# Pair grams in fp32, one sample in a quarter of the array, in place of split fp32r grams of four samples

## The chip, the cores and the metric
The kernel runs on one core of one Trainium2 chip. The metric is the device time of one execution in microseconds. The times shown are medians of a few executions, and the profile is of one more execution, whose own time is given beside its span.

## The reference
The program is a recommendation model: dot products between all pairs of 27 feature vectors of a sample, followed by a small multilayer perceptron. Biases are not zero.

```python
# bottom_output (2048, 27, 128), bottom_mlp_output (2048, 128), all float32
dots  = jnp.einsum('bfd,bgd->bfg', bottom_output, bottom_output)
pairs = dots[:, tril_i, tril_j]                    # 351 pairs below the diagonal
x = jnp.concatenate([bottom_mlp_output, pairs, zeros(B, 1)], axis=1)   # 480 columns
for w, b in ((w0, b0), (w1, b1), (w2, b2), (w3, b3)):   # 480 -> 1024 -> 1024 -> 512 -> 256
    x = jax.nn.relu(x @ w.T + b)
return x @ w_out.T + b_out                          # (2048, 1)
```

## The kernel before
The batch is cut into 8 chunks of 256 samples. A chunk passes through the four layers with its samples as the 256 moving columns of each product (`products`, L776). Each layer product is made of three fp32r products: high weights by high activations, low weights by high activations, high weights by low activations (`ALL`; `HIGH` is the first two). A chunk has 136 tile products of each kind, 408 matmuls. ScalarE drains an accumulator with bias and relu (`drain`, L891), VectorE rounds the result to fp32r (`split_high`, L1022), and GpSimd subtracts to get the low part (`split_low`, L626).

While a chunk goes through the layers, the pair products ("grams") of the next chunk are made beside it. A gram is the 27 x 27 matrix of dot products of one sample. Four samples are a group, four groups a unit, 16 units a chunk. A unit goes through this chain:

- SP loads its rows (`load_rows`, L500), in four DMAs of 32-row blocks, arranged so that VectorE's transposes of 32 x 32 blocks turn them whole.
- VectorE transposes (`turn_raw`, L977) into `raw`, with features in the columns: 128 partitions (the 128 dimensions) x 512.
- ScalarE rounds to fp32r (`turned_hi`, L863); VectorE subtracts for the low part (`turned_lo`, L982; in chunk 0 every second unit's is on GpSimd, L619).
- TensorE makes four products, one a group (`gram`, L735): the weights are the high parts of 4 samples in 128 columns, the moving columns are 4 x 28 of the high parts and as many of the low parts. That computes all cross products of four samples, of which only the four diagonal 27 x 27 blocks are wanted. Each unit takes two banks of PSUM, and there are two such pairs (`GRAM_RING`, `GRAM_BANKS`).
- ScalarE copies three of the four samples' blocks, high by high and high by low, out of PSUM into `parts` (`gram_parts`, L875), VectorE the fourth (`gram_parts_rest`, L1004).
- VectorE transposes the high-by-low parts (`turn_low`, L1015), GpSimd adds them twice, once as they are and once transposed (`add_parts`, L605 and L612), into `grams`.

When the 16 units of a chunk are there, SP spills `grams` to memory (`spill`, L447) and gathers the wanted pairs back as 351 rows of 256 samples (`gather`, L452). They are split into high and low parts at the end of the chunk (`pairs_hi`, L901, `pairs_lo`, L1050).

The first chunk's grams come ahead of everything (`first_steps`). There the rows are turned by TensorE (`turn_early`, L691), copied by ScalarE (L848), and each group's gram is one plain fp32 product of 108 columns by 128 weight columns (`gram_early`, L715). ScalarE and VectorE share the copies out of PSUM (`early_move`, L856, `early_rest`, L991). Then the weights are transposed by TensorE (`turn_weights`, L686) through the same PSUM banks and split by ScalarE (L840) and VectorE (L968). Some of that stands in the middle of chunk 0.

The order of the work is written out once for all engines. `chunk_steps` makes a list of steps, and each engine runs through the same list and does its own part. `hooks_of` gives small lists of steps ("hooks") that are put in after every 18 matmuls of the layers (`HOOK`; in chunk 0 after every 6, a unit every second hook). What a hook holds is made by `unit_steps(n, ahead)`: the transpose of unit n, the split of unit n - 1, the gram of unit n - 3 and the sum of unit n - 4. The first five hooks' worth of a chunk stand at the end of the chunk before it (`AHEAD`), so a chunk c does most units of chunk c + 1 and begins those of c + 2. Each engine executes its instructions in order, with semaphore waits between them. Chunk 7 has no grams beside it.

Of the kernel before, what the change touches and what calls it, by code (L numbers as in the profile page):

```python
# [14 lines left out]
P = 128  # L15
# [39 lines left out]
ACC_RING, GRAM_RING, TURN_RING = 3, 2, 2  # L55
GRAM_BANKS = 2

XT_RING, XT_LAG = 4, 2
assert ACC_RING + 1 + GRAM_RING * GRAM_BANKS == 8

# [9 lines left out]
EVEN = FEATS + 1  # L70
EARLY_SLOTS, SHORT_LAG = 8, 2
RAW_RING = 2
EARLY_XT = 2 * XT_RING
EARLY_BY_ACT = [1] * (UNITS - 4) + [2] * 4
QUADS_BY_ACT = 3
# [59 lines left out]
def unit_steps(n, ahead):  # L135


    steps, g = [], n - 1 - XT_LAG
    if n < UNITS:
        steps.append(("raw", ahead, n))  # L140
    if 1 <= n <= UNITS:
        steps.append(("turn", ahead, n - 1))
    if g >= 1:
        steps.append(("sum", ahead, g - 1))
    if g >= 0:
        steps.append(("gram", ahead, g))
    if g == UNITS - 1:
        steps.append(("sum", ahead, g))
    return steps


UNIT_HOOKS = UNITS + XT_LAG + 1
# [92 lines left out]
def dlrm_program(nc, x, x_mlp, w0, b0, w1, b1, w2, b2, w3, b3, w_out, b_out, y):  # L245
    weights = [w0, w1, w2, w3]
    biases = [b0, b1, b2, b3]
    with ExitStack() as ctx:
# [28 lines left out]
        raw = sb("raw", [P, RAW_RING, UNIT_GROUPS, GROUP * QUAD])  # L277
        mlp_rows = sb("mlp_rows", [P, 2, P])
        xt_full, = shared(("xt_full", [P, EARLY_XT, UNIT_GROUPS, GROUP * QUAD]))
        xt = sb("xt", [P, XT_RING, UNIT_GROUPS, 2, GROUP * QUAD], F32R)  # L280
        parts = sb("parts", [P, 2, 2, UNIT_GROUPS, QUAD])
        low_t = sb("low_t", [P, 2, UNIT_GROUPS, QUAD])
# [11 lines left out]
        gram_ps = ctx.enter_context(nc.psum_tensor("gram_ps", [P, GRAM_RING * GRAM_BANKS, 512], F32))  # L294
# [13 lines left out]
        grams_zeroed = sem("grams_zeroed")  # L308
        xt_zeroed = sem("xt_zeroed")
        parts_zeroed = sem("parts_zeroed")  # L310
# [4 lines left out]
        raw_turned = sem("raw_turned")  # L315
        xt_hi_done = sem("xt_hi_done")
        xt_done = sem("xt_done")
        xt_odd_done = sem("xt_odd_done")
        gram_done = sem("gram_done")
        early_moved = sem("early_moved")  # L320
        parts_done = sem("parts_done")
        parts_rest_done = sem("parts_rest_done")
        low_turned = sem("low_turned")
        sum_done = sem("sum_done")
# [60 lines left out]
        def weight_bank(n):  # L385

            return gram_ps[:, n % (GRAM_RING * GRAM_BANKS), :] if n < LATE_WEIGHTS else side_ps[:, :]

# [5 lines left out]
        def by_pool(d, u):  # L394

            return isinstance(d, int) and d == 1 and u % 2 == 1

        def wait_xt(engine, d, u):

            if isinstance(d, int) and u < 0:  # L400
                d, u = d - 1, u + UNITS
            if by_pool(d, u):
                engine.wait_ge(xt_odd_done, u // 2 + 1)
            elif isinstance(d, int) and d <= 1:
                engine.wait_ge(xt_done, d * UNITS + (u // 2 if d else u) + 1)
            else:
                engine.wait_ge(xt_done, d * UNITS - UNITS // 2 + u + 1)

        def xt_part(u, h):

            return xt[:, u % XT_RING, :, h, :].rearrange("p j (s f) -> p j s f", s=GROUP)[:, :, :, 0:FEATS]

        def early_xt(u):

            return xt_full[:, u % EARLY_XT].rearrange("p j (s f) -> p j s f", s=GROUP)[:, :, :, 0:FEATS]

        def early_gram(u, s):

            found = gram_ps[quad_of(s), u % (GRAM_RING * GRAM_BANKS), 0:UNIT_COLS].rearrange("p (j n) -> p j n", j=UNIT_GROUPS)
            return found[:, :, FEATS * s:FEATS * (s + 1)]  # L420

        def gram_place(u, s):

            return grams[quad_of(s), :, u * UNIT_GROUPS:(u + 1) * UNIT_GROUPS].rearrange("p g j -> p j g")

        def raw_cols(u):

            return raw[:, u % RAW_RING].rearrange("p j (s f) -> p j s f", s=GROUP)[:, :, :, 0:FEATS]

# [3 lines left out]

        def quad_of(s):

            return slice(QUAD * s, QUAD * s + FEATS)

        def gram_found(u, s):

            b = u % GRAM_RING * GRAM_BANKS  # L440
            found = gram_ps[quad_of(s), b:b + GRAM_BANKS, :].rearrange("p a (b n) -> p (a b) n", n=2 * P)
            return found[:, :, 0:2 * GROUP * EVEN].rearrange("p j (h n) -> p h j n", h=2)[
                :, :, :, EVEN * s:EVEN * s + FEATS]

# [32 lines left out]
        def _(sp):  # L477
# [28 lines left out]
            def spill(d, quads=range(GROUP)):  # L506


                sp.wait_ge(grams_done, d * UNITS + UNITS)
                if isinstance(d, int) and d == 0:  # L510
                    sp.wait_ge(early_moved, UNITS)
                for s in quads:
                    spill_quad(sp, s)
# [68 lines left out]
        def _(pool):  # L582
# [6 lines left out]
            nc.gpsimd.memset(grams[:], 0.0).then_inc(grams_zeroed, 1)  # L589
# [8 lines left out]

            def add_parts(d, u):

                n = (d - 1) * UNITS + u + 1
                hh, hl = parts[:, u % 2, 0], parts[:, u % 2, 1]
                pool.wait_ge(parts_done, n)
                pool.wait_ge(parts_rest_done, n)
                nc.gpsimd.tensor_tensor(hh, hh, hl, ALU.add).then_inc(sum_done, 1)  # L605

                pool.wait_ge(sum_done, n)
                pool.wait_ge(low_turned, n)
                if u == 0:

                    pool.wait_ge(spilled, d * GROUP * 16)
                nc.gpsimd.tensor_tensor(  # L612
                    grams[:, :, u * UNIT_GROUPS:(u + 1) * UNIT_GROUPS].rearrange("p g j -> p j g"),
                    parts[:, u % 2, 0, :, 0:FEATS], low_t[:, u % 2, :, 0:FEATS], ALU.add).then_inc(grams_done, 1)

            def turned_lo(d, u):

                pool.wait_ge(xt_hi_done, (d - 1) * UNITS + u + 1)
                nc.gpsimd.tensor_tensor(xt_part(u, 1), raw_cols(u), xt_part(u, 0).bitcast(F32),  # L619
                                        ALU.subtract).then_inc(xt_odd_done, 1)  # L620
# [8 lines left out]
            def chunk(c):  # L629
                for step in steps_of(c):  # L630
                    if step[0] == "mm":
                        _, layer, m, _, k1, parts = step
                        if k1 == K_TILES[layer] and 2 in parts and layer < 3:
                            split_low(c, layer, m)
                    elif step[0] == "turn" and by_pool(c + step[1], step[2]):
                        turned_lo(c + step[1], step[2])
                    elif step[0] == "sum":
                        add_parts(c + step[1], step[2])
# [9 lines left out]
        def _(pe):  # L648
            def turn_weights(n):

                g, bank, ring = ORDER[n], weight_bank(n), GRAM_RING * GRAM_BANKS
                if n < ring:

                    pe.wait_ge(early_moved, UNITS + 1 - ring + n)
# [48 lines left out]
            def gram_early(u):  # L703


                pe.wait_ge(xt_done, u + 1)
                if u == 0:
                    pe.wait_ge(xt_zeroed, 1)
                ring = GRAM_RING * GRAM_BANKS
                if u >= ring:  # L710

                    pe.wait_ge(early_moved, u + 1 - ring)
                    pe.wait_ge(grams_done, u + 1 - ring)
                for j in range(UNIT_GROUPS):
                    last = nc.tensor.matmul(gram_ps[:, u % ring, j * GROUP_ROWS:(j + 1) * GROUP_ROWS],  # L715
                                            xt_full[:, u % EARLY_XT, j, :], early_xt(u)[:, j], start=True, stop=True)
                last.then_inc(gram_done, 1)

            def gram(d, u):

                wait_xt(pe, d, u)
                if isinstance(d, int) and d == 1 and u < GRAM_RING:
                    if u == 0:

                        pe.wait_ge(w_done, LATE_WEIGHTS)
                        pe.wait_ge(xt_zeroed, 2)
                else:

                    pe.wait_ge(parts_done, (d - 1) * UNITS + u + 1 - GRAM_RING)
                    pe.wait_ge(parts_rest_done, (d - 1) * UNITS + u + 1 - GRAM_RING)  # L730
# [83 lines left out]
            for step in first_steps():  # L814
                if step[0] == "turn":
                    turn_early(step[1])
                elif step[0] == "early":
                    gram_early(step[1])
# [13 lines left out]
        def _(act):  # L832
# [10 lines left out]
            def early_copy(u):  # L843
                act.wait_ge(turned, u + 1)
                if u >= EARLY_XT:

                    act.wait_ge(gram_done, u + 1 - EARLY_XT)
# [273 lines left out]
```

## Time and profile before

| | us |
|---|---|
| median of 3 runs | 517.59 (516.37 to 517.98) |
| the profiled execution | 519.78 |
| its span, first to last instruction | 518.0 |
| first and last instruction of the early grams' matmuls on TensorE | 5.6 to 28.2 |
| one steady chunk | 57 |
| mean granted TensorE clock, share of full | 0.984 |
| DMA traffic | 53.24 MB |

The kernel before is also measured beside every later run. A row of a group has the line of the kernel, the engine (PE is TensorE's matmul, PEld its weight load, DVE is VectorE, ACT ScalarE, POOL GpSimd, SP SyncE, with a q for the sequencer that issues DMAs), the operation, what it writes and reads, the shapes and the count. Behind the first bar stand the busy time in us and the mean ns of one; behind the second the time for which the engine was idle just before them, and what ended it. Matmuls overlap in the pipeline, so that their busy time is less than count times mean, and the distance from one start to the next is the cost of one. Weight loads overlap with matmuls.

### The profile page before, as it was taken

What the parts mean: (1) busy time and instruction counts of PE and PEld (TensorE: products, weight loads), DVE (VectorE), ACT (ScalarE), POOL (GpSimd) and SP (SyncE); (2) the same over time, 40 slices, a digit from 0 to 9 for tenths busy, and PEclk for the clock granted to TensorE, in tenths of its full rate; (3) what the DMA queues carried; (4) which work ended last, traced back from release to release, by engine and by line L of the source; (5) the groups of instructions that cost most, each with busy time, mean ns of one, the idle gap of its engine ahead of it and who ended that gap; (6) DMA issues with size and microseconds to landing.
All of it is one profiled execution on the core that took longest, in us unless ns stands there. A gap on an engine that the chain in (4) does not pass through costs nothing.

```text
span 518.0 us, 13822 instructions
## 1 busy us (share of the span) xinstructions
PE 495.9 (96%) x4075; PEld 488.7 (94%) x4075; DVE 322.2 (62%) x742; ACT 295.9 (57%) x736; POOL 263.9 (51%) x475
## 2 busy tenths in 40 slices
PE   6986998898999999999999999999999999999998
PEld 6975997898999999999999999999999999999997
DVE  3764778665884788648974788458874788332110
ACT  4654677853864577637773586547763686433112
POOL 2710377632865367624864287626764386524221
PEclk9986999998999999999999999999999999999999
DMA  8997877447673566347663666266653762210000
GB/s 220 235 307 163 261 120 120 69 93 119 98 110 72 106 113 100 62 107 120 102 101 68 113 106 106 50 124 113 101 81 83 129 96 41 57 41 2 1 1 0
DMA packets 281055, 53.24 MB, mean 103 GB/s; under 512 B 265126, under 2 KB 279230, under 8 KB 281022
## 3 DMA queue, kind: packets, MB, share of 16 engines
q1 hardware_dynamic: 279090, 52.22, 53.2%
q10 hardware_dynamic: 1932, 0.61, 0.5%
q8 instruction: 17, 0.28, 0.2%
q14 instruction: 16, 0.13, 0.1%
HBM read 45.71 MB, written 7.09 MB: 102 GB/s over the span
## 4 chain that ended last, share of the span: by engine, by line
PE 79%; DMA 6%; issue 4%; POOL 3%; SPq 3%; ACT 3%; DVE 1%; ACTq 0%; POOLq 0%; DVEq 0%
PE acc L776 67%; PE gram_ps L735 8%; DMA blocks<-grams 2%; DMA rows<-in_r_bottom_output_dram 2%; PE gram_ps L715 2%; DMA pairs<-blocks 1%; ACT parts L875 1%; POOL parts L605 1%; SPq L482 1%; ACT h_full L891 1%; PE gram_ps L686 1%; POOL grams L612 1%; POOL xt L619 1%; SPq L447 1%; SPq L452 1%
## 5 line engine op out<-in xcount | busy, mean ns | idle before, releaser
L776 PE MATMUL acc<-h_a,w_hi 128*128 128x256 f32 x1152 | 223.7, 285 | 3.4 <-DVE h_a L1022 2.4
L776 PEld LDWEIGHTS acc<-h_a,w_hi 128*128 128x128 f32 x1152 | 185.2, 191 | 5.2 <-DVE h_a L1022 3.0
L891 ACT ACTIVATE h_full<-acc,small_t 128x256 f32<-128x256 f32 x175 | 82.9, 473 | 148.0 <-PE acc L776 146.6
L776 PE MATMUL acc<-h_a,w_lo 128*128 128x256 f32 x576 | 158.7, 282 | 0.0
L626 POOL TENSOR_TENSOR h_a<-h_full,h_a 128x256 fp32r<-128x256 f32 x96 | 72.2, 752 | 135.0 <-DVE h_a L1022 135.0
L875 ACT ACTIVATE parts<-gram_ps 27x216 f32<-27x216 f32 x336 | 114.4, 340 | 41.3 <-PE gram_ps L735 27.6
L776 PEld LDWEIGHTS acc<-h_a,w_lo 128*128 128x128 f32 x576 | 110.2, 191 | 0.0
L776 PE MATMUL acc<-x,w_hi 128*128 128x256 f32 x504 | 102.8, 291 | 2.4 <-ACT x L901 2.4
L776 PE MATMUL acc<-h_b,w_hi 128*128 128x256 f32 x512 | 97.2, 284 | 0.0
L776 PEld LDWEIGHTS acc<-x,w_hi 128*128 128x128 f32 x504 | 84.4, 197 | 3.4 <-ACT x L901 3.1
L977 DVE STREAM_TRANSPOSE raw<-rows 128x512 f32<-128x512 f32 x112 | 78.9, 704 | 7.4 <-DMA rows<-in_r_bottom_output_dram 4.2
L626 POOL TENSOR_TENSOR h_b<-h_full,h_b 128x256 fp32r<-128x256 f32 x64 | 47.4, 740 | 69.9 <-DVE h_b L1022 69.9
L776 PEld LDWEIGHTS acc<-h_b,w_hi 128*128 128x128 f32 x512 | 81.6, 191 | 0.0
L605 POOL TENSOR_TENSOR parts<-parts 128x128 f32<-128x128 f32 x112 | 77.5, 692 | 5.6 <-DVE parts L1004 5.1
L982 DVE TENSOR_TENSOR xt<-raw,xt 128x432 fp32r<-128x432 f32 x104 | 74.6, 717 | 1.0 <-ACT xt L863 1.0
L776 PE MATMUL acc<-x,w_lo 128*128 128x256 f32 x252 | 72.0, 289 | 0.0
L1022 DVE CAST h_a<-h_full 128x256 fp32r<-128x256 f32 x96 | 30.2, 314 | 64.1 <-ACT h_full L891 62.4
L776 PE MATMUL acc<-h_b,w_lo 128*128 128x256 f32 x256 | 70.0, 283 | 0.0
L735 PE MATMUL gram_ps<-xt 128*128 128x224 f32 x448 | 67.9, 274 | 0.3 <-POOL xt L619 0.3
L863 ACT ACTIVATE xt<-raw 128x432 fp32r<-128x432 f32 x112 | 62.6, 559 | 2.7 <-DVE raw L977 2.2
L1022 DVE CAST h_b<-h_full 128x256 fp32r<-128x256 f32 x64 | 18.8, 294 | 67.9 <-ACT h_full L891 67.7
L612 POOL TENSOR_TENSOR grams<-parts,low_t 128x108 f32<-128x108 f32 x112 | 47.9, 427 | 25.3 <-DVE low_t L1015 13.4
(67 smaller groups left out, 488.7 us busy)
## 6 DMA issues: line engine op xcount, KB each, us to landing
rows<-in_r_bottom_output_dram SPq DMA_DIRECT2D x444, 64.0 KB, 2.1
blocks<-grams SPq DMA_DIRECT2D x30, 216.0 KB, 4.0
w_raw<-in_L_rec_w_dram SPq DMA_DIRECT2D x6, 1024.0 KB, 7.3
early_rows<-in_r_bottom_output_dram SPq DMA_DIRECT2D x12, 224.0 KB, 6.1
stage_pairs<-in_L_rec_w_dram SPq DMA_DIRECT2D x1, 1408.0 KB, 10.2
w_raw<-in_L_rec_w_dram SPq DMA_DIRECT2D x2, 512.0 KB, 8.9
mlp_rows<-r_bottom_mlp_output_dram SPq DMA_DIRECT2D x8, 128.0 KB, 2.2
pairs<-blocks SPq DMA_DIRECT2D x8, 126.0 KB
```

Source lines behind the costliest of these rows:

```text
L605: nc.gpsimd.tensor_tensor(hh, hh, hl, ALU.add).then_inc(sum_done, 1)
L612: nc.gpsimd.tensor_tensor(grams[:, :, u * UNIT_GROUPS:(u + 1) * UNIT_GROUPS].rearrange("p g j -> p j g"), parts[:, u % 2, 0, :, 0:FEATS], ...
L626: nc.gpsimd.tensor_tensor(h[:, m, 1, :], h_full[:, slot % 2, :], h[:, m, 0, :].bitcast(F32), ALU.subtract).then_inc(split_done, 1)
L715: last = nc.tensor.matmul(gram_ps[:, u % ring, j * GROUP_ROWS:(j + 1) * GROUP_ROWS], xt_full[:, u % EARLY_XT, j, :], early_xt(u)[:, j], st ...
L735: last = nc.tensor.matmul(found, xt[:, u % XT_RING, j, 0], both, start=True, stop=True)
L776: last = nc.tensor.matmul(acc_slot(c, slot), weight(wp, layer, m, k), in_tile(layer, k, xp), start=(k == 0 and n == 0), stop=(k == K_TILES ...
L863: nc.scalar.activation(xt_part(u, 0), raw_cols(u), ACT.Copy).then_inc(xt_hi_done, 1)
L875: last = nc.scalar.activation(parts[quad_of(s), u % 2, :, :, 0:FEATS], gram_found(u, s), ACT.Copy)
L891: nc.scalar.activation(h_full[:, slot % 2, :], acc_slot(c, slot), ACT.Relu, bias=small_t[:, slot:slot + 1]).then_inc(drained, 1)
L977: nc.vector.transpose(raw[:, u % RAW_RING].rearrange("p j n -> p (j n)"), rows[:, r].rearrange("p j n -> p (j n)")).then_inc(raw_turned, 1)
L982: nc.vector.tensor_tensor(xt_part(u, 1), raw_cols(u), xt_part(u, 0).bitcast(F32), ALU.subtract).then_inc(xt_done, 1)
L1022: nc.vector.tensor_copy(h[:, m, 0, :], h_full[:, slot % 2, :]).then_inc(high_done, 1)
```

## The change
All grams, the early ones too, become plain fp32 products of one sample: the weights are that sample's 32 columns (27 features and 5 zeros), the moving columns its 27 features, and the product is placed in the 32-column quarter of the array that ends in the sample's 32 partitions of PSUM. A unit becomes 16 products in one bank (`GRAM_RING` is 4 banks now), and its gram leaves the bank in one copy of 128 x 108 elements, by ScalarE in the steady chunks and by VectorE in the early ones. VectorE's transpose writes straight into `xt`, a ring of 8. `raw`, `parts`, `low_t`, `xt_full`, the split of x, the sum on GpSimd, the memset of `grams` and their semaphores are gone. A hook holds the transpose of unit n and the gram of unit n - 1, so a chunk needs 17 hooks in place of 19. In a chunk's first unit ScalarE waits for the spill of the chunk before it, as GpSimd did.

```diff
-ACC_RING, GRAM_RING, TURN_RING = 3, 2, 2
-GRAM_BANKS = 2
-
-XT_RING, XT_LAG = 4, 2
+ACC_RING, GRAM_RING, TURN_RING = 3, 4, 2
+
+XT_RING, XT_LAG, UNIT_LAG = 8, 2, 1
...
-    steps, g = [], n - 1 - XT_LAG
+    steps = []
     if n < UNITS:
         steps.append(("raw", ahead, n))
-    if 1 <= n <= UNITS:
-        steps.append(("turn", ahead, n - 1))
-    if g >= 1:
-        steps.append(("sum", ahead, g - 1))
-    if g >= 0:
-        steps.append(("gram", ahead, g))
-    if g == UNITS - 1:
-        steps.append(("sum", ahead, g))
+    if n >= UNIT_LAG:
+        steps.append(("gram", ahead, n - UNIT_LAG))
     return steps
...
+        def samples(u):
+            return xt[:, u % XT_RING].rearrange("p j (s f) -> p j s f", s=GROUP)[:, :, :, 0:FEATS]
+        def gram_found(u):
+            return gram_ps[:, u % GRAM_RING, 0:P].rearrange("p (j f) -> p j f", f=QUAD)[:, :, 0:FEATS]
+        def gram_place(u):
+            return grams[:, :, u * UNIT_GROUPS:(u + 1) * UNIT_GROUPS].rearrange("p g j -> p j g")
...
-                    sp.wait_ge(raw_turned, (d - 1) * UNITS + u + 1 - ROWS_RING)
+                    sp.wait_ge(xt_done, d * UNITS + u + 1 - ROWS_RING)
...
+            def gram(d, u):
+                pe.wait_ge(xt_done, d * UNITS + u + 1)
+                if isinstance(d, int) and d == 0 and u == 0:
                     pe.wait_ge(xt_zeroed, 1)
...
+                elif not (isinstance(d, int) and d == 0 and u < GRAM_RING):
+                    pe.wait_ge(grams_done, d * UNITS + u + 1 - GRAM_RING)
                 for j in range(UNIT_GROUPS):
-                    at = j % 2 * 2 * P
-                    found = gram_ps[:, u % GRAM_RING * GRAM_BANKS + j // 2, at:at + 2 * GROUP * EVEN]
-                    both = xt[:, u % XT_RING, j].rearrange("p h (s f) -> p (h s) f", f=QUAD)[:, :, 0:EVEN]
-                    last = nc.tensor.matmul(found, xt[:, u % XT_RING, j, 0], both, start=True, stop=True)
+                    for s in range(GROUP):
+                        at = slice(QUAD * s, QUAD * (s + 1))
+                        last = nc.tensor.matmul(gram_found(u)[at, j], xt[:, u % XT_RING, j, at], samples(u)[:, j, s],
+                                                start=True, stop=True, tile_position=(0, QUAD * s))
                 last.then_inc(gram_done, 1)
...
+            def move_gram(d, u):
+                act.wait_ge(gram_done, d * UNITS + u + 1)
                 if u == 0:
+                    act.wait_ge(spilled, d * GROUP * 16)
+                nc.scalar.activation(gram_place(u), gram_found(u), ACT.Copy).then_inc(grams_done, 1)
...
+                dve.wait_ge(gram_done, d * UNITS + u + 1 - XT_RING)
+                nc.vector.transpose(xt[:, u % XT_RING].rearrange("p j n -> p (j n)"),
+                                    rows[:, r].rearrange("p j n -> p (j n)")).then_inc(xt_done, 1)
+            def early_move(u):
                 dve.wait_ge(gram_done, u + 1)
+                nc.vector.tensor_copy(gram_place(u), gram_found(u)).then_inc(grams_done, 1)
```

## Rows read from the trace of the kernel before

**Rows 1.** The page's head: busy time of each engine over the whole span.
```profile
PE 495.9 (96%) x4075; PEld 488.7 (94%) x4075; DVE 322.2 (62%) x742; ACT 295.9 (57%) x736; POOL 263.9 (51%) x475
```

**Rows 2.** By stretch: length, busy PE, PEld, DVE, ACT, POOL; clock, DMA share, GB/s.
```profile
62.00:121.00 59.00, 52.71 (x436) 51.03 (x434) 41.25 (x93) 40.43 (x103) 34.45 (x56) 1.00 0.62 105
121.00:178.00 57.00, 56.41 (x463) 56.35 (x464) 39.24 (x90) 33.27 (x85) 32.52 (x52) 0.97 0.56 97
...
406.00:463.00 57.00, 56.80 (x478) 56.49 (x477) 35.01 (x84) 32.88 (x86) 32.21 (x51) 1.00 0.41 73
```

**Rows 3.** The chain of waits: start us, us, what; early units, first spill, steady chunk.
```profile
18.06 0.89 PE gram_ps L715 x8
...
25.81 2.69 PE gram_ps L715 x24
...
30.09 8.53 DMA blocks<-grams
...
171.72 2.87 PE acc L776 x24
```

**Rows 4.** Timeline of TensorE's matmuls: start us, us from first start to last end.
```profile
199.77 0.60 PE L735 MATMUL gram_ps<-xt 128*128 128x224 f32 x4
200.21 0.29 PE L776 MATMUL acc<-h_a,w_hi 128*128 128x256 f32 x1
...
202.37 0.60 PE L735 MATMUL gram_ps<-xt 128*128 128x224 f32 x4
```

**Rows 5.** Groups of instructions by line, costliest first: busy us, mean ns, idle before.
```profile
L776 PE MATMUL acc<-h_a,w_hi 128*128 128x256 f32 x1152 | 223.7, 285 | 3.4 <-DVE h_a L1022 2.4 <-ACT h_full L891 1.0
...
L875 ACT ACTIVATE parts<-gram_ps 27x216 f32<-27x216 f32 x336 | 114.4, 340 | 41.3 <-PE gram_ps L735 27.6 <-POOL grams L612 10.3
...
L891 ACT ACTIVATE h_full<-acc,small_t 128x256 f32<-128x256 f32 x175 | 82.9, 473 | 148.0 <-PE acc L776 146.6
...
L977 DVE STREAM_TRANSPOSE raw<-rows 128x512 f32<-128x512 f32 x112 | 78.9, 704 | 7.4 <-DMA rows<-in_r_bottom_output_dram 4.2 <-POOL xt L619 2.6
...
L863 ACT ACTIVATE xt<-raw 128x432 fp32r<-128x432 f32 x112 | 62.6, 559 | 2.7 <-DVE raw L977 2.2
...
L715 PE MATMUL gram_ps<-xt_full 128*128 128x108 f32 x128 | 18.3, 293 | 0.0
...
L856 ACT ACTIVATE grams<-gram_ps 27x108 f32<-27x108 f32 x20 | 7.0, 350 | 6.8 <-PE gram_ps L715 6.7
...
L750 PE MATMUL side_ps<-ident,mlp_rows 128*128 128x128 f32 x16 | 3.0, 272 | 0.0
...
L791 PE MATMUL side_ps<-h_full,small_t 128*1 128x256 f32 x4 | 1.0, 377 | 0.2 <-ACT h_full L891 0.2
...
L791 PEld LDWEIGHTS side_ps<-h_full,small_t 128*1 128x1 f32 x4 | 0.2, 80 | 0.7 <-issue 0.4 <-ACT h_full L891 0.3
```

**Rows 6.** The chain of waits in chunk 0: start us, us, what.
```profile
82.76 0.96 POOL xt L619
...
108.06 4.03 DMA blocks<-grams
```

**Rows 7.** Timeline of the weight loads at the end of the kernel.
```profile
514.67 0.11 PEld L791 LDWEIGHTS side_ps<-h_full,small_t 128*1 128x1 f32 x2 [0.35 <-issue]
515.09 0.13 PEld L791 LDWEIGHTS side_ps<-h_full,small_t 128*1 128x1 f32 x2 [0.30 <-ACT h_full L891]
```

**Rows 8.** Timeline of all engines at the start of one steady unit.
```profile
199.65 0.28 PE L776 MATMUL acc<-h_a,w_hi 128*128 128x256 f32 x1
199.65 0.19 PEld L735 LDWEIGHTS gram_ps<-xt 128*128 128x128 f32 x1
```

**Rows 9.** Timeline of matmuls where transposes stand between products.
```profile
171.34 0.38 PE L750 MATMUL side_ps<-ident,mlp_rows 128*128 128x128 f32 x2
171.47 0.36 PE L776 MATMUL acc<-h_b,w_hi 128*128 128x256 f32 x1
171.67 0.28 PE L776 MATMUL acc<-h_b,w_lo 128*128 128x256 f32 x1
```

More of the change, by code:

```diff
@@ L385, in weight_bank @@
         def weight_bank(n):
[L387 removed]
+            return gram_ps[:, n % GRAM_RING, :] if n < LATE_WEIGHTS else side_ps[:, :]
         def raw_rows(n):
@@ L634, in chunk @@
                             split_low(c, layer, m)
[L635 to L638, printed above, removed]
             chunk(0)
@@ L701, in turn_early @@
                 turn_rows(u, early_rows_of(u))
-            def gram_early(u):
-                pe.wait_ge(xt_done, u + 1)
-                if u == 0:
+            def gram(d, u):
+                pe.wait_ge(xt_done, d * UNITS + u + 1)
+                if isinstance(d, int) and d == 0 and u == 0:
                     pe.wait_ge(xt_zeroed, 1)
[L709 to L721, printed above, removed]
                 if isinstance(d, int) and d == 1 and u < GRAM_RING:
@@ L817, in _ @@
                 elif step[0] == "early":
-                    gram_early(step[1])
+                    gram(0, step[1])
                 elif step[0] == "weights":
@@ L916, in chunk @@
                             drain(c, layer, m)
-                    elif step[0] == "turn":
-                        turned_hi(c + step[1], step[2])
                     elif step[0] == "gram":
-                        gram_parts(c + step[1], step[2])
+                        move_gram(c + step[1], step[2])
                     elif step[0] == "weights":
@@ L932, in _ @@
                     early_copy(step[1])
-                elif step[0] == "early":
-                    early_move(step[1])
                 elif step[0] == "spill":
                     act.wait_ge(grams_done, UNITS)
-                    act.wait_ge(early_moved, UNITS)
                     for s in (2, 3):
@@ L985, in early_rest @@
-            def early_rest(u):
-                dve.wait_ge(gram_done, u + 1)
-                if u == 0:
-                    dve.wait_ge(grams_zeroed, 1)
-                for s in range(EARLY_BY_ACT[u], GROUP):
-                    last = nc.vector.tensor_copy(gram_place(u, s), early_gram(u, s))
-                last.then_inc(grams_done, 1)
-            def gram_parts_rest(d, u):
-                dve.wait_ge(gram_done, d * UNITS + u + 1)
-                if isinstance(d, int) and d == 1 and u < 2:
-                    dve.wait_ge(parts_zeroed, 1)
-                else:
-                    dve.wait_ge(grams_done, d * UNITS + u - 1)
-                for s in range(QUADS_BY_ACT, GROUP):
-                    last = nc.vector.tensor_copy(parts[quad_of(s), u % 2, :, :, 0:FEATS], gram_found(u, s))
-                last.then_inc(parts_rest_done, 1)
@@ L1007, in turn_low @@
-            def turn_low(d, u):
-                n = (d - 1) * UNITS + u + 1
-                dve.wait_ge(parts_done, n)
-                dve.wait_ge(parts_rest_done, n)
-                if not (isinstance(d, int) and d == 1 and u < 2):
-                    dve.wait_ge(grams_done, d * UNITS + u - 1)
-                nc.vector.transpose(low_t[:, u % 2].rearrange("p j g -> p (j g)"),
-                                    parts[:, u % 2, 1].rearrange("p j g -> p (j g)")).then_inc(low_turned, 1)
+                dve.wait_ge(gram_done, d * UNITS + u + 1 - XT_RING)
@@ L1063, in chunk @@
                         turn_raw(c + step[1], step[2])
-                    elif step[0] == "turn" and not by_pool(c + step[1], step[2]):
-                        turned_lo(c + step[1], step[2])
-                    elif step[0] == "gram":
-                        gram_parts_rest(c + step[1], step[2])
-                    elif step[0] == "sum":
-                        turn_low(c + step[1], step[2])
                     elif step[0] == "weights":
@@ L1075, in chunk @@
                         pairs_lo(c + step[1])
-            nc.vector.memset(xt_full.rearrange("p r j (s f) -> p (r j s) f", f=QUAD)[:, :, FEATS:], 0.0).then_inc(xt_zeroed, 1)
-            nc.vector.memset(parts[:], 0.0).then_inc(parts_zeroed, 1)
+            nc.vector.memset(xt.rearrange("p r j (s f) -> p (r j s) f", f=QUAD)[:, :, FEATS:], 0.0).then_inc(xt_zeroed, 1)
             for step in first_steps():
                 if step[0] == "early":
-                    early_rest(step[1])
+                    early_move(step[1])
                 elif step[0] == "weights":
```

117 lines of the change are left out of this document (8 added, 109 removed).

## Prediction
> **What bounds the kernel now.** I read the page's head first: TensorE is busy 96% of the span, the other engines 51 to 62% [rows 1]. A busy share alone does not say that TensorE sets the time, so I took the busy time by stage next [rows 2]. In a steady chunk of 57 us (there are six, from 121 to 463 us) TensorE is busy 56.4 to 56.8; from 62 to 121 it idles 6.3 us (59.0 less 52.7); before that it waits for the first transfers. From 463 us on there are no grams, and nothing there changes. The granted clock is 0.97 to 1.00 in these rows.
>
> The chain of waits [rows 3] confirms it: in a steady chunk it runs through L776 and L735 on TensorE, a product of 256 columns taking 0.120 us (24 in 2.87). The timeline shows the grams of one unit from 199.77 to 200.21, then 18 products to 202.37, then the next unit [rows 4]. **A unit costs 0.44 us of TensorE; with 18 products of 0.12 it makes the period of 2.60 us.** All that the other engines do per unit lies beside it. So the question is whether 16 small fp32 products fit into 0.44 us.
>
> **The change, part by part.** From the other engines it takes much. Per unit ScalarE loses 0.56 + 3 x 0.34 us [rows 5], VectorE three of its four instructions, GpSimd both. ScalarE gains one copy out of a bank, 128 x 108 elements; the nearest row is L856, the same layout on 27 partitions, 0.35 us. All of it lies under a period of 2.6 us and is worth only the stalls that those engines cause: the 6.3 us of idle TensorE in chunk 0, where the chain passes GpSimd's L619 [rows 6], and some 0.2 us per steady chunk. Part of chunk 0's idle time belongs to weight turning, which stays. I take 6 us, bounds 0 and 8. The dropped memset of grams lies ahead of a wait for weights, and is worth nothing; so is the shorter evacuation after the last early gram, under the rounding.
>
> On TensorE the trace has one thing to go by: an fp32 product is issued as two loads and two matmuls (128 records at L715 for the 64 products of 16 units [rows 5]). So a unit becomes 32 load/matmul pairs in place of 4. **What does a pair cost?** Three limits follow from rows.
>
> (a) Streaming. L791 (256 columns, fp32) takes 0.377 us a record where L776 (256 columns, fp32r) takes 0.285 [rows 5]. The 0.092 more is near the 0.107 of another 256 columns at 2.4 GHz, so an fp32 pass streams at about two cycles a column, and 27 columns take 54 / 2.4 = 22.5 ns.
>
> (b) Loading. At L715 eight pairs take 0.89 us, 0.111 each [rows 3], although by (a) their 108 columns stream in 0.090. So the load of 128 columns bounds there. Two cycles a column are 0.107, so 0.004 is fixed, and 32 columns need 64 / 2.4 + 4 = 31 ns.
>
> (c) The turn from one set of weights to the next. With one weight column, at L791, the second load starts 0.03 us after the first in one pair and 0.05 in the other: 0.11 and 0.13 less a record of 0.08 [rows 5, 7]. The matmul starts between them.
>
> (b) and (c) say 31 to 33 ns; a straight line from (c)'s first pair to (b)'s 128 columns says 33 + 31 x 0.61 = 52. I take 33, since a fixed 33 ns added to a rate of 0.83 ns a column would overshoot the measured 0.111. The last gram is followed by a load of 128 columns that a matmul of 22 ns can't cover: 0.11 once. **Unit: 31 x 0.033 + 0.111 = 1.13 us, against 0.44: +0.69.**
>
> That happens 7 x 16 = 112 times: +77 us. The 16 early units take 0.89 us each (8 records' steps) [rows 3]: +0.24 each, exposed for the nine from 18 us on, where TensorE carries the chain: +2.2. The seven before lie beside the arriving rows.
>
> Moved waits. The gram now waits for a transpose of one hook earlier (0.70 us, L977), before for a split of two hooks earlier. TensorE queues everything behind that wait, and reaches the next hook after 2.16 + 1.13 = 3.3 us; in that time VectorE must see a drain (0.47), cast it and transpose, under 2 us together: hidden. In chunk 0 a unit comes every 12 products, 2.6 us, beside the weight copies; at worst the saving there is lost, which is the bound of 0. Before a chunk's first gram is copied, ScalarE instead of GpSimd now waits for the spill, and its drains queue behind. That spill starts after unit 15, six hooks earlier, and lands in 4 to 8.5 us [rows 3, 6]: hidden. SP's row loads wait for the same transposes as before, and neither SP nor GpSimd issues another DMA.
>
> The sum: 519.8 (profiled; span 518.0) + 77 + 2.2 - 6 = 593. The median of 517.6 is 2.2 lower, so 590.8, **590 us**.
>
> **Two rules beside the rows.** Between a transpose by the array (L750) and a 256-column product the timeline shows no stop: the second L750 starts at 171.44 (0.38 less 0.27 [rows 5] after 171.34), the second product at 171.67, and 0.23 is just their two steps, 0.11 and 0.12 [rows 9]. The sum therefore charges nothing for a change of shape. The Trainium skill, "TensorEngine Tiling (Array Packing)", section Tiling Modes, says that changing the tiling mode drains TensorE; no row of before enters a tiling mode, so the trace can't confirm it. Two such changes a unit are rival 3.
>
> The closest matmul starts of these rows are 171.44 and 171.47. The Trainium skill, "TensorE: Matmul & The Clock Gate", section Back-to-back issue gap, puts the least start-to-start at about 25 ns, which agrees; by it even perfectly overlapped quarters would need 31 x 0.025 + 0.11 = 0.89 us a unit, an estimate of 562 in all. With matmuls decoded in software it gives 62 ns each, an estimate of 2.03 us a unit and some 700 in all.
>
> **The rivals.**
> 1. *Quarters overlap.* Another quarter loads and streams while one works; only the turn from first to second pass within a product stays serial. 16 x 0.033 + 0.08 = 0.61 us a unit: +0.17 x 112 = 19, early -2.5, stalls -6: 528. Half way to the serial case, at 0.87 us: 560. For it: the four products of a group share nothing but x. Against: a load starts only when the matmul before it does, both at 199.65 [rows 8]. Chance 0.22. The same page on the clock gate, Part 3, says that tiles run concurrently.
> 2. *Serial*, as summed: 0.36.
> 3. *Each change of array shape drains.* A record at L776 lasts 0.285, of which 0.107 is streaming, so 0.18 is the way through the array. Twice a unit 0.36; for 121 units +44: 634. Chance 0.17.
> 4. *The turn grows with the columns*, 52 ns a pair: 1.72 us a unit, +143, early +7.5, -6: 662. A lower granted clock in stretches of narrow products would land here too. Chance 0.12.
> 5. *A 32-column load takes as long as 128 columns*, the quarter buying nothing: 32 x 0.111 = 3.55 a unit, +348, +24, -6: 884. Chance 0.04.
> 6. *Faster.* All quarters run at once through both passes: 32 x 0.033 / 4 + 0.08 = 0.34 us. TensorE saves 0.10 x 112 + 0.55 x 9, and 6 of stalls: 495. It decides once a unit takes less than about 0.52 us (112 x 0.08 = 6 + 9 x 0.37), near 13 ns a pair, less than half of any step between starts shown above. Chance 0.06; between this and rival 1 lies no change, 0.03.
>
> **The numbers.** Within 0.3%, 1.6 us, a measurement here can't tell a change from none. Slower 0.36 + 0.22 + 0.17 + 0.12 + 0.04 = 0.91, same 0.03, faster 0.06. The range takes in rivals 1 and 3 and the lower part of 4: 530 to 655 us. Below it lie rival 6, no change and the very end of rival 1 (0.10), above it rival 5 and half of rival 4 (0.10).
>
> **What would show it.** In the changed profile: a steady chunk of some 68 us (57 + 16 x 0.69) in place of 57; 3584 + 512 matmul records for grams; in the timeline 1.1 us from a unit's first gram to the next product, matmul starts 0.033 apart, and a first product that comes a full load late. Rival 1 would show starts 33 and then a few ns apart in turn; rival 3 a hole of 0.18 us before and after the grams; rival 4 even steps of 50 ns. TensorE stays busy in over 97% of a steady chunk, ScalarE falls to a third or less. The idle time of chunk 0 should be nearly gone. I am wrong if a steady chunk takes under 60 us, or if TensorE waits for VectorE's transposes.

## The result and the profile after

The changed kernel takes 541.2 us (539.35 to 542.35), the kernel before 516.98 beside it: a ratio of 1.045, 95% interval 1.041 to 1.049. The direction was forecast; the size was not: +24 us in place of +73, and made of other parts.

The page's head of the kernel after, to set against [rows 1]: TensorE has nearly twice the matmul records (7595 against 4075) and only 13 us more busy time, while the other three engines have lost about half of theirs, as expected.

```profile
PE 508.7 (94%) x7595; PEld 479.5 (89%) x7595; DVE 171.5 (32%) x384; ACT 166.6 (31%) x380; POOL 132.8 (25%) x242
```

Busy time by stage, the same view as [rows 2] (length, then busy PE, PEld, DVE, ACT, POOL, the granted clock, DMA):

```profile
62.00:121.00 59.00, 58.08 (x1033) 54.54 (x1034) 26.96 (x52) 22.35 (x51) 11.26 (x15) 1.00 0.68 118
...
182.00:243.00 61.00, 58.63 (x924) 55.54 (x923) 19.43 (x44) 17.77 (x43) 15.00 (x20) 1.00 0.55 94
243.00:304.00 61.00, 60.22 (x924) 57.10 (x924) 17.87 (x40) 17.08 (x42) 14.97 (x20) 0.97 0.54 91
```

Chunk 0 is nearly full now: 0.9 us idle in that window where it was 6.3. But a steady window, which was full before, has a hole of 2.4 us. The chain of waits gives the length of a chunk from the one pair of transposes in each (start us, us, what):

```profile
168.09 0.22 PE side_ps L642 x2
...
229.90 0.22 PE side_ps L642 x2
...
293.35 0.22 PE side_ps L642 x2
...
356.31 0.22 PE side_ps L642 x2
```

That is 61.8, 63.5 and 63.0 us, against 56.9 to 57.2 before; I had forecast 68. The waits of TensorE and the timeline at the start of a chunk name the hole:

```profile
PE acc L668 <- issue: 11.6, 4, 3.1
```
```profile
178.18 0.64 PE L668 MATMUL acc<-h_a,w_hi 128*128 128x256 f32 x4
181.74 0.38 PE L668 MATMUL acc<-x,w_hi 128*128 128x256 f32 x1 [2.92 <-issue]
```

The last product of chunk 1 and the first of chunk 2 are 3 us apart, and "issue" says that nothing which the profile shows was waited for. There are four such holes, and a loop of five iterations turns four times. A unit of grams, in the timeline of the matmuls, against [rows 4]:

```profile
200.40 0.28 PE L668 MATMUL acc<-h_a,w_hi 128*128 128x256 f32 x1
200.61 0.45 PE L626 MATMUL gram_ps<-xt 128*32 128x27 f32 x32
200.99 0.39 PE L668 MATMUL acc<-h_a,w_hi 128*128 128x256 f32 x1
201.22 0.28 PE L668 MATMUL acc<-h_a,w_lo 128*128 128x256 f32 x1
```

From the last product before the grams to the second one after them are 0.82 us; less two steps of 0.12, **the unit costs 0.58 us**. The same reading of before (199.65 to 200.34) gives 0.45. And inside the 0.58 the 32 matmuls are all started within 0.45 - 0.19 = 0.26 us (the record of one is 192 ns here), 8.4 ns from start to start. The rest is at the edges: 0.09 us between the end of the product's step (200.52) and the first gram, and 0.12 from the last gram's start (200.87) to 200.99, where the full-width product's load begins; that load then takes its 0.11 uncovered.

So two things were to be explained: 8.4 ns where I had 33, and holes that I hadn't foreseen.

### The profile page after: what moved, and what is told of

Read it like the earlier page. It is cut to its first block, busy times and chain, and to the rows that moved or that the text cites. A ratio compares the mean times of both kernels' runs of the same rounds, so it can differ in the third digit from the quotient of the medians.

```text
span 539.3 us, 18870 instructions
## 1 busy us (share of the span) xinstructions
PE 508.7 (94%) x7595; PEld 479.5 (89%) x7595; DVE 171.5 (32%) x384; ACT 166.6 (31%) x380; POOL 132.8 (25%) x242
## 4 chain that ended last, share of the span: by engine, by line
PE 84%; DMA 7%; SPq 4%; issue 2%; DVE 1%; ACT 1%; ACTq 0%
PE acc L668 73%; PE gram_ps L626 8%; DMA rows<-in_r_bottom_output_dram 4%; SPq L439 2%; DMA pairs<-blocks 2%; DMA blocks<-grams 1%; SPq L421 1%; PE gram_ps L594 1%; DVE xt L844 1%; PE side_ps L599 1%; ACT h_full L763 1%; PE acc L599 1%; PE side_ps L689 0%; PE side_ps L594 0%; PE side_ps L642 0%
## 5 line engine op out<-in xcount | busy, mean ns | idle before, releaser
L668 PE MATMUL acc<-x,w_hi 128*128 128x256 f32 x504 | 107.9, 301 | 15.6 <-issue 11.6
L668 PE MATMUL acc<-h_b,w_hi 128*128 128x256 f32 x512 | 101.2, 289 | 0.0
L844 DVE STREAM_TRANSPOSE xt<-rows 128x512 f32<-128x512 f32 x112 | 77.7, 702 | 13.8 <-DMA rows<-in_r_bottom_output_dram 13.8
L856 DVE CAST h_a<-h_full 128x256 fp32r<-128x256 f32 x96 | 28.2, 294 | 149.8 <-ACT h_full L763 149.8
L748 ACT ACTIVATE grams<-gram_ps 128x108 f32<-128x108 f32 x112 | 41.0, 368 | 90.8 <-PE gram_ps L626 90.8
L626 PEld LDWEIGHTS gram_ps<-xt 128*32 128x32 f32 x4096 | 47.3, 117 | 22.3 <-issue 6.6
L626 PE MATMUL gram_ps<-xt 128*32 128x27 f32 x4096 | 61.2, 200 | 3.4 <-issue 1.5
L668 PEld LDWEIGHTS acc<-x,w_lo 128*128 128x128 f32 x252 | 50.6, 201 | 0.0
L668 PEld LDWEIGHTS acc<-h_b,w_lo 128*128 128x128 f32 x256 | 49.0, 191 | 0.0
L594 PE MATMUL gram_ps<-ident,w_raw 128*128 128x128 f32 x96 | 15.0, 295 | 3.2 <-DVE w_lo L835 2.0
```

What stands on the lines that cost most here:

```text
L594: last = nc.tensor.transpose(bank[:, k * P:(k + 1) * P], src[:, at:at + P], ident[:])
L626: last = nc.tensor.matmul(gram_found(u)[at, j], xt[:, u % XT_RING, j, at], samples(u)[:, j, s], start=True, stop=True, tile_position=(0, Q ...
L668: last = nc.tensor.matmul(acc_slot(c, slot), weight(wp, layer, m, k), in_tile(layer, k, xp), start=(k == 0 and n == 0), stop=(k == K_TILES ...
L748: nc.scalar.activation(gram_place(u), gram_found(u), ACT.Copy).then_inc(grams_done, 1)
L844: nc.vector.transpose(xt[:, u % XT_RING].rearrange("p j n -> p (j n)"), rows[:, r].rearrange("p j n -> p (j n)")).then_inc(xt_done, 1)
L856: nc.vector.tensor_copy(h[:, m, 0, :], h_full[:, slot % 2, :]).then_inc(high_done, 1)
```

## The experiments

**1. Are the holes code that is fetched again?** Theory 1: at the turn of TensorE's loop its instructions must be loaded anew, because the body has become too long. In a_unroll TensorE's loop over chunks 1 to 5 is written out as straight code, nothing else changes; b_unroll is the same edit of the kernel before.

```diff
-            with pe.Fori(1, CHUNKS - 2) as c:
+            for c in range(1, CHUNKS - 2):
                 chunk(c)
```

> The changed kernel with TensorE's loop over chunks 1 to 5 written out as straight code; every other engine keeps its loop. Theory 1 (code): the four holes of 3.0 to 3.4 us on TensorE, each at the turn of the loop and each ended by 'issue', are TensorE's instructions being fetched again, since the loop body no longer stays loaded. Then they vanish, 4 x 3.1 = 12.4 us, with the slow-clock stretches behind them perhaps 1 to 3 more: 526 to 529 us, and the instruction queue moves no more than the program's length once. Rival (data): the holes are a wait for the chunk's first input or for another engine, which only falls there. Then they stay and the time stays near 541.

> Control: the kernel before with the same loop written out on TensorE alone. Theory 1: its body stays loaded, it has no such hole (0.48 us at most at the turn), so the time stays at 517, within 1.5 us, against before. Rival: straight code is faster for another reason (register waits, branches): it gains some us here too, and the gain of the other run is no sign of fetching.

Measured: a_unroll 525.4 us, ratio 1.013 [1.007, 1.020] to before; b_unroll 519.0 beside 518.3, ratio 1.000 [0.997, 1.004]. The changed kernel gains 15.8 us from straight code, the kernel before nothing. A chunk of a_unroll lasts 58.64 us, with no hole:

```profile
226.97 0.22 PE side_ps L642 x2
...
285.61 0.22 PE side_ps L642 x2
```

The gain is more than the four holes (3.2, 3.4, 2.9 and 3.2 us from start to start, 12 us over the usual step), because behind three of them TensorE ran slowly for a while. Behind the second hole, which ends at 243.8 us, the granted clock stands at half (the last but two of the numbers), and the chunk lengths that hold such a stretch are 63.0 to 63.5 us, not 61.8:

```profile
245.20:248.40 3.20, 3.20 (x45) 2.92 (x44) 0.95 (x2) 0.84 (x2) 0.73 (x1) 0.50 0.00 1
```

**2. Is it the turn itself, or only what straight code changes beside it?** a_hint keeps the loop and its register waits, and adds one hint to TensorE at the top of each iteration that the loop will branch back. b_double takes the kernel before, with its old grams, and puts two chunks into the loop's body.

```diff
-            with pe.Fori(1, CHUNKS - 2) as c:
+            with nc.Fori(1, CHUNKS - 2, engines=bass.OrderedEngineSet([pe.engine]), hint_back_edge=True) as c:
```
```diff
-            with pe.Fori(1, CHUNKS - 2) as c:
-                chunk(c)
+            with pe.Fori(1, CHUNKS - 3, 2) as c:
+                chunk(c)
+                chunk(c + 1)
+            chunk(CHUNKS - 3)
```

> The changed kernel, loop kept, with one hint on TensorE at the top of each iteration that the loop will branch back to its start. Same instructions otherwise. Theory 1 (fetching at the turn): the four holes of 3.1 us shrink to some 0.5 us or nothing, a steady chunk goes from 63 to 58.6 to 59 us, as with straight code, and the whole to 525 to 528 us. Rival: the gain of straight code came from the constant waits or from the missing loop counter, and the fetching was no cause; then the hint does nothing or costs a little, 541.

> The kernel before with two chunks in TensorE's loop body (two iterations, chunk 5 after it), so that its body is about as long as the changed kernel's, with the old work. Theory 1: at the one turn of the loop stands a hole of some 3 us that the kernel before hasn't: 520 to 521 us. Rival (the holes belong to the narrow products or to the transposes of the changed kernel): no hole, 517 to 518.

Measured: a_hint 530.0 (ratio 1.024 [1.019, 1.028]), b_double 526.3 (1.015 [1.010, 1.020]), beside 517.9. Both took longer than forecast (525 to 528, and 520 to 521), and both still decide against their rivals. With the hint the chunks in the loop take 58.64 us like straight code. Most of what it takes over the forecast stands behind the loop: nine products into chunk 6, the code after the last iteration, is a hole (2.5 us from start to start) with a slow stretch behind it, and the length that holds both is 62.0 us:

```profile
416.27 0.28 PE L668 MATMUL acc<-x,w_hi 128*128 128x256 f32 x1
418.80 0.97 PE L668 MATMUL acc<-x,w_hi 128*128 128x256 f32 x3 [2.25 <-issue]
```

In b_double, the one turn has two holes, with a granted clock of 0.50 from 242.2 to 248.8 us, and more time is lost than forecast (timeline of matmuls):

```profile
238.35 0.76 PE L776 MATMUL acc<-h_a,w_hi 128*128 128x256 f32 x5
242.18 0.58 PE L776 MATMUL acc<-x,w_hi 128*128 128x256 f32 x1 [3.08 <-issue]
...
245.29 0.37 PE L776 MATMUL acc<-x,w_lo 128*128 128x256 f32 x1 [2.10 <-issue]
```

There are no narrow products in that kernel. The row of the instruction queue on the profile's page agrees (packets, MB, share). These are its rows in the kernels before, after, a_hint and b_double:

```profile
q8 instruction: 17, 0.28, 0.2%
```
```profile
q8 instruction: 67, 1.10, 0.8%
```
```profile
q8 instruction: 31, 0.51, 0.4%
```
```profile
q8 instruction: 36, 0.59, 0.5%
```

A packet is 16 KB. a_unroll moves 60 of them for its 15190 loads and matmuls, some 253 each. The loop's body has 924 matmuls (408 products, 512 for the grams, 4 more) with a load each, 1848 in all or 7.3 packets; the body of the kernel before has 476, so 952. The changed kernel moves 36 packets more than the same program with the hint, nine a turn, so its body was read again at every turn. One such packet falls into the first hole (the queue between 178.85 and 181.74 us), and one into the hole of a_hint (416.3 to 418.8):

```profile
q8 instruction: 1, 0.02, 2.1%
```
```profile
q8 instruction: 1, 0.02, 2.4%
```

Between 165 us and that hole a_hint reads no packet at all, and neither does the kernel before between 181 and 422 us. So the long body of 1848 did stay loaded over the loop's turns once the hint was there, and **its length alone is not the cause**. Up to 178.8 us, about the first turn, the changed kernel had read 21 packets and the hinted one 20, which served it through the whole loop and nine products beyond. So the 21st is code from behind the loop. That reading on pushes the loop's start out is argued from this and not shown. a_unroll moves 60 packets and has no hole at all: reading as such costs nothing here, and what costs is that at a branch it starts late. The row of one of a_unroll's chunks (its counts take in what runs at the edges of the window):

```profile
240.64:299.28 58.64, 58.64 (x926) 55.75 (x925) 19.42 (x45) 17.79 (x44) 14.98 (x21) 1.00 0.57 97
```

**Theory 1 stands in this form:** the body is read again at the turn if it is long and nothing tells TensorE that it will branch back. The Trainium skill, "Runtime: NRT & Kernel Launch", section Instruction fetch mechanics, says that TensorE holds 2048 instructions, fetched in blocks of 256, and that a taken branch whose target isn't in the current window of two pages stalls for a fetch. The trace agrees on the 16 KB and on the stall, but not on two pages: bodies of 952 and, with the hint, of 1848 were not read again. That a body below 2048 can miss, and that a miss costs 3 us, is what these runs show.

**3. Why does a pair take 8 ns?** In a_swap_unroll the 16 products of a unit come quarter by quarter; on the base of a_unroll.

```diff
-                for j in range(UNIT_GROUPS):
-                    for s in range(GROUP):
+                for s in range(GROUP):
+                    for j in range(UNIT_GROUPS):
```

> The changed kernel with straight code and the 16 products of a unit in the other order: all four products of one quarter, then the next quarter's, so that 8 pairs in a row use one quarter. Theory 3: a pair takes only 8 ns because neighbouring products are in different quarters and overlap, and my 33 ns for the turn of weights holds within one quarter. Then a pair takes 25 to 33 ns, a unit 0.5 to 0.8 us more, a steady chunk 67 to 71 us in place of 58.6, the whole 583 to 614 us. Rival: narrow loads and matmuls are simply short, wherever they are; then nothing changes, 525.

Measured 571.3 us (ratio 1.104 [1.097, 1.110]), 46 more than a_unroll for the order alone, though less than the 58 at least that I expected; the chunks take 65.69 us, 7.05 more or 0.44 a unit:

```profile
245.82 0.22 PE side_ps L642 x2
...
311.51 0.22 PE side_ps L642 x2
```
```profile
200.76 0.90 PE L626 MATMUL gram_ps<-xt 128*32 128x27 f32 x32
```

32 pairs now take 0.90 - 0.19 = 0.71 us, 22.9 ns each. That this is near the 22.5 ns that the prediction gave to streaming is chance, as the starts inside the stretch show. Here are its first 3, first 5 and first 9 matmuls (the view cut at 200.86, 200.915 and 201.00 us):

```profile
200.76 0.28 PE L626 MATMUL gram_ps<-xt 128*32 128x27 f32 x3
200.76 0.34 PE L626 MATMUL gram_ps<-xt 128*32 128x27 f32 x5
200.76 0.40 PE L626 MATMUL gram_ps<-xt 128*32 128x27 f32 x9
```

From the third to the fifth, all in one quarter, a step is 0.03 us (32 ns in the trace). After the fifth, four more start in 0.06 us: the next quarter has begun while the first finishes its eight. So matmuls of one quarter are serial, at 32 ns, and **the four quarters run beside each other**, in this order only where one quarter's row ends and the next begins. The order of the changed kernel has the same step within a quarter (its stretch cut after 9 and after 17 matmuls):

```profile
200.61 0.28 PE L626 MATMUL gram_ps<-xt 128*32 128x27 f32 x9
200.61 0.34 PE L626 MATMUL gram_ps<-xt 128*32 128x27 f32 x17
```

Eight matmuls, two for each quarter, start in 0.06 us. That is my 33 ns for the turn of weights, right within one quarter in both orders, and paid by four at once. What it consists of, streaming, loading or both, no run here separates.

**4. What do the edges of a stretch cost?** Theory 2: what a unit pays beyond its 0.26 us is entering and leaving the quarter mode. Then grams of two or four units in one stretch, at every second or fourth hook, save it without touching any product.

```diff
-    if n >= UNIT_LAG:
-        steps.append(("gram", ahead, n - UNIT_LAG))
+    if n and n % 4 == 0:
+        steps += [("gram", ahead, u) for u in range(n - 4, n)]
```

> The changed kernel with the grams of four units in one stretch at every fourth hook, in place of one unit at each; the same products, copies and loads. Theory 2 (switch): a unit costs TensorE about 0.58 us, of which 32 pairs take only 0.27 (0.0084 us a pair) and 0.31 are the entry into and the way out of the quarter mode. With 28 stretches in place of 112 the 84 missing switches give back 84 x 0.31 = 26 us: 515 us, the loop's holes still there. Rival (pairs): the cost is per product, and nothing changes: 541. If ScalarE's four copies in a row delay a drain, some of it comes back as new idle time before a product, up to 1 us per stretch.

> Both edits together. If theories 1 and 2 are right and independent: 541 - 12 - 26 = 503 us, 14 faster than before. If one holds alone, 515 or 529.

> Straight code and grams of two units in one stretch: the middle point between one unit (steady chunk 58.64 us) and four (55.5). Theory 2 with a price per switch of 0.26 us (12 switches for 3.1): 4 fewer switches than ... 8 in place of 16 give 58.64 - 8 x 0.26 = 56.5 us a chunk, and 511 to 514 in all. Rival: what four units gained is the longer time to work ahead (fewer waits), and two give less or more than in proportion.

Measured: a_batch4 529.1 (ratio 1.018 [1.011, 1.025]), a_batch4_unroll 507.0 (0.978 [0.972, 0.984]), a_batch2_unroll 511.6 (0.988 [0.983, 0.994]). The chunk lengths are the clean measure, with one, two and four units a stretch: 58.64, then

```profile
221.73 0.22 PE side_ps L642 x2
...
278.19 0.22 PE side_ps L642 x2
```

56.46 for two, and for four

```profile
219.95 0.22 PE side_ps L642 x2
...
275.51 0.22 PE side_ps L642 x2
```

55.56. With 16, 8 and 4 stretches, the first 8 switches saved are worth 2.18 us and all 12 worth 3.08: 0.27 and 0.26 each. **Theory 2 stands, at 0.26 us a switch pair**, a little under the 0.32 that the timeline's edges add up to. It is the whole price of an edge pair, with the 0.11 us of the uncovered load in it. A stretch of four takes 1.35 us for 128 pairs, 9.1 ns each and not 8.4, which takes a little of the saving back:

```profile
193.90 1.35 PE L626 MATMUL gram_ps<-xt 128*32 128x27 f32 x128
```

a_batch4 alone gained only 12 of the 26 us that I expected. At the measured price 84 switches are worth 22; in chunk 0 TensorE waited 6.7 us for transposes whose rows came late; the turns of the loop had holes of 3.2 to 3.7 us, 1 us more in all. Some 2 us remain. Behind those waits the granted clock is at half for a while, which it is nowhere in chunk 0 of the changed kernel (0.91 and 1.00 for 62 to 121 us); that can hold the rest, though I didn't split it:

```profile
73.00:82.50 9.50, 6.50 (x89) 6.32 (x90) 3.64 (x6) 1.58 (x4) 0.73 (x1) 0.50 0.71 111
```

With straight code the same step gains 18.4 us (525.4 to 507.0) of the 22; chunk 0 waits 4.3 us for transposes there and 2.8 in a_unroll, and again there is a stretch at half the clock behind the waits (75 to 81 us). The forecast for both edits was 503.

**5. Chunk 0 and the early stage.** a_mixed_unroll has stretches of four, but of one in chunk 0. a_wide_early restores the wide early grams with their copies by two engines (`gram_early`, `early_move`, `early_rest`). Its expectation was written for the changed kernel as base; the kernel that ran has a_mixed_unroll as its base, so its time is to be read against that.

```diff
-        hooks[place] += unit_steps(u, 1)
+        hooks[place] += unit_steps(u, 1, 1)
```
```diff
-                    gram(0, step[1])
+                    gram_early(step[1])
```

> Straight code, grams of four units in one stretch as in a_batch4_unroll, but in chunk 0 one unit at a time, since there TensorE waited 4.3 us for transposes whose rows came late. If that wait is what four units cost there, chunk 0 loses it and pays 12 more switches of 0.26 us (3.1): 506 to 508 us, no more than 1 us better than 507.0. If the one-unit order of chunk 0 waits as long for the same rows, it is 3 us slower, 510.

> The changed kernel with the 16 early units alone as before: four fp32 products of 128 weight columns a unit, copied out by ScalarE and VectorE. Theory 4 (clock): with narrow grams TensorE stays at 1.2 GHz through the early stage (transposes 0.18 us apart in every run with narrow early grams, 0.092 in the kernel before from 10 us on). With wide ones the transposes go back to 0.09, the last early gram ends at 28.5 us in place of 30.1. The first product still waits for spill and gather, so the whole gains 0 to 2 us: 539 to 541. Rival: the slow transposes follow from the switch of array shape before them, not from the clock; with wide grams there is no switch in this stage, so they'd go back too, but then a transpose in the steady part right after narrow grams would be slow as well.

Measured: 506.9 and 506.9 us (0.979 [0.974, 0.983] and 0.980 [0.975, 0.984]); neither differs from a_batch4_unroll. In a_mixed_unroll the waits for transposes are gone from chunk 0, and its 12 more switches cost about as much, as expected. In a_wide_early the early stage looks different. The chain of waits of the changed kernel, to be set against [rows 3]:

```profile
20.26 0.92 PE acc L599 x4
21.17 0.58 PE gram_ps L626 x32
```

and that of a_wide_early:

```profile
19.88 0.37 PE acc L614 x4
20.25 0.89 PE gram_ps L636 x8
```

The grams of a unit are quicker by 0.31 us, and the four transposes beside them slower by 0.55. In after, a_unroll, a_hint and a_mixed_unroll, with narrow early grams, the transposes started 0.18 us or more apart for most of this stage, in the runs with wide ones 0.092 from 10 us on; 0.18 against 0.092 is the ratio of 1.2 to 2.4 GHz. The granted clock says the same where it is on record, here for after and for a_wide_early:

```profile
16.50:30.00 13.50, 11.63 (x344) 9.27 (x332) 3.05 (x9) 4.12 (x8) 11.49 (x72) 0.50 0.96 271
```
```profile
16.50:30.00 13.50, 12.05 (x113) 11.88 (x113) 9.28 (x27) 8.74 (x22) 11.46 (x72) 1.00 1.10 280
```

In a_unroll the transposes changed to 0.093 at 24.6 us with the same neighbours as before, so the switch of shape is not the cause, and the clock is. The mean that the table prints for 0 to 30 us can hide this: it is 1.00 in a_unroll, whose transposes were slow up to that point. Why narrow grams leave the clock low stays open, and they don't always: in a_swap_unroll, whose stretches are narrow too but last longer, it was 1.00 from 9.5 to 19 and from 23 to 30 us. It costs little here: the early grams end at 30.1 us in after and at 28.5 in before, but the first product that needs the gathered pairs starts at 48.24 and 48.02. The medians of a_mixed_unroll and a_wide_early are the same, though the early grams end at 31.4 in one and at 29.3 in the other.

## Why the prediction was wrong

**The sum was 590; the kernel takes 541.** Per unit it charged 1.02 us for the pairs and 0.11 for a load; measured are 0.26 for the pairs, the same 0.11, and 0.21 at the edges. Over 112 units that is 85 us too much and 24 too little, and the turns of the loop, 16 us, were missing. So 541 lies inside the stated range of 530 to 655 by luck: two misses that point up made up for part of the one that points down. Point by point:

- *TensorE bounds the kernel, and the other engines' relief is worth some 6 us*: right, as far as a remainder can show. Chunk 0's idle time went from 6.3 to 0.9 us. a_unroll is 7.1 us over before, while its units cost 112 x (0.58 - 0.45) = 14.6 more; the difference of 7.5 is near that relief.
- *An fp32 product is two pairs*: right, 4096 records at L626.
- *A pair takes 33 ns*: right within one quarter, where it takes 32 in either order. The 22.5 ns of streaming by themselves no run shows; the mean of 22.9 with the order swapped is partly overlapped quarters.
- *Pairs follow each other serially*: **this is the step that failed.** "I take 33" was multiplied by 31. Quarters overlap fully, both passes, and 32 pairs take 0.26 us, which is the 32 x 0.033 / 4 of rival 6, given 0.06. My argument against it, that a load starts only when the matmul before it does [rows 8], was read from full-width weights, which leave no other quarter free; it said nothing of quarters. It is the 0.76 us a unit above, 85 us in all.
- *No charge for a change of shape*: also wrong. The row with transposes between products [rows 9] is no change of tiling. Entering and leaving cost 0.26 us by the chunk lengths, 0.32 by the timeline; 0.11 of it is the load that the sum had, so 0.15 to 0.21 were missing, 17 to 24 us in all. Rival 3 had 0.36. The Trainium skill's rule that a change of tiling mode drains TensorE ("TensorEngine Tiling (Array Packing)", section Tiling Modes) agrees with these numbers. The rivals were treated as exclusive, but 3 and 6 held together: 0.34 + 0.36 would have given 0.70 a unit where 0.58 was measured, and a total near 540 without the holes, where a_unroll took 525.
- *The 25 ns between starts* (the Trainium skill, "TensorE: Matmul & The Clock Gate", section Back-to-back issue gap) do not hold for quarters: 8.4 ns. The estimate of 562 built on it fell, and so did the one of 700.
- *The loop*: **a term of 16 us is missing from the sum.** I had counted 4096 records and not asked where the 1848 loads and matmuls of a loop's body are kept. The trace of before had a hint of it: 17 instruction packets for a program that takes 32 as straight code (b_unroll), so its body was kept and not read again.
- *Early stage, 2.2 us*: not borne out. A unit's grams are 0.31 us quicker and its transposes 0.55 slower, at the lower clock; that the difference is the 0.24 which the sum charged for slower grams is luck. The early grams end 1.6 us later, and the first product that needs their pairs starts 0.2 us later.
- *Moved waits hidden*: right. In steady chunks TensorE never waits for a transpose (in chunk 0 it does, 0.3 us in after and 2.8 in a_unroll); in a_unroll a chunk of 58.64 us is busy throughout. The prediction had named its own sign of being wrong, a steady chunk under 60 us; a_unroll shows one, and in the changed kernel the holes hid it (61.8 to 63.5).

## What to carry to other kernels

Price narrow products by how many quarters work at once, and order them so that neighbours lie in different quarters; then gather them into few long stretches, since each entry into the quarter mode and out of it cost 0.26 us here, in stretches of 32 to 128 pairs. When an edit multiplies instructions in a loop, count the body on the engine that bounds: here 952 loads and matmuls turned without a hole, and 1848 paid 3 us at each turn and mostly a slow clock behind it. Straight code had no such cost, and the hint on the way back left one hole behind the loop. With quarters in rotation, stretches of four and straight code, a_batch4_unroll runs in 507.0 us, 2.2% under the kernel before (95% interval 1.6 to 2.8%) and 6% under the changed one.

## What the runs showed of the hardware that I had not expected

- Two fp32 passes in the four quarters overlap down to 8.4 ns from start to start; the same 32 pairs sorted by quarter take 22.9 ns each. Within one quarter the step is 32 ns in both orders.
- Entering and leaving the quarter mode: 0.26 us from the chunk lengths, with 0.09 us visible before and 0.12 plus an uncovered load of 0.11 after.
- A turn of the loop with a body of 1848 loads and matmuls: 2.9 to 3.4 us. With the hint the same body stays loaded, and one hole of 2.5 us stands behind the last iteration. A body of two old chunks had two holes at one turn, 7.6 us in all with the slow clock behind them (64.53 us for a chunk of 56.9).
- With narrow fp32 grams between transposes the granted clock was 0.50 in most of the early stage (1.2 GHz), with wide ones 1.00; with the narrow ones sorted by quarter it was mostly 1.00 too. In the steady part, between full-width products, the transposes and products ran at full speed, but for the stretches behind the holes.
